# Selective scan plus mixture of experts on one core: softplus moved from TensorE to VectorE, one state group kept in PSUM

## The reference, cut to what matters

```python
uo = x @ W_in.T;  u, o = uo[..., :256], uo[..., 256:]
u = silu(depthwise_conv4(u) + conv_b)
g = u @ W_gate.T                        # 64 delta_lo, 16 b, 16 c
delta = softplus(delta_lo @ W_delta.T + delta_bias)
A = -exp(A_log)
h = exp(A * delta_t) * h + (delta_t * u_t) * b_t     # 256 channels x 16 states, 256 positions
y_t = sum_s h * c_t
y = (y + D * u) * sigmoid(o) * o
x = x + y @ W_out.T
# second block: 8 experts, top 2 (softmax), SwiGLU of width 176, and a shared SwiGLU of width 352
```

## Time and profile before

| | |
|---|---|
| median of 3 runs | 1453.29 us (1452.8 to 1456.53) |
| the profiled execution | 1453.74 us, its span 1451.6 us |
| mean granted TensorE clock | 0.961 of full speed |
| busy: TensorE, VectorE, ScalarE, GpSimd | 1273.9, 1042.5, 1080.1, 1219.0 us |
| period of a full step | 41.47 us (scan(7) starts at 640.42 and again at 681.89) |
| full steps (k = 2 to 29) | 28 |

### The profile page before, as it was taken

The page is one execution under the profiler, slowest core; times in us unless marked ns, Lnnn a source line. Parts: engine busy times, 40 slices in busy tenths (PEclk is TensorE's granted clock), DMA queues, the critical chain, the costliest instruction groups (busy, mean ns, idle before and its releaser), DMA issues.

```text
span 1451.6 us, 26176 instructions
## 1 busy us (share of the span) xinstructions
PE 1273.9 (88%) x9203; PEld 950.7 (65%) x9203; DVE 1042.5 (72%) x1664; ACT 1080.1 (74%) x2219; POOL 1219.0 (84%) x568
## 2 busy tenths in 40 slices
PE   3455999999999999999999999999999999998888
PEld 2223766777667667776676677766766777665677
DVE  2245778877777788777777887777778877776753
ACT  3777778777877787778777877787778777876642
POOL 3299898898889988988899889888998898899920
PEclk8667999999999999999999999999999999999989
DMA  3433322333333223333332233333322333233000
GB/s 102 103 89 84 92 67 69 95 96 92 74 86 95 65 70 96 96 93 75 84 94 66 70 96 96 92 74 85 95 65 69 96 97 92 69 83 89 7 5 8
DMA packets 71486, 115.08 MB, mean 79 GB/s; under 512 B 8174, under 2 KB 30396, under 8 KB 71356
## 3 DMA queue, kind: packets, MB, share of 16 engines
q1 hardware_dynamic: 67180, 110.71, 30.2%
q10 hardware_dynamic: 4176, 2.70, 0.6%
HBM read 41.04 MB, written 5.24 MB: 32 GB/s over the span
## 4 chain that ended last, share of the span: by engine, by line
PE 34%; DVE 22%; ACT 17%; issue 16%; POOL 1%; DVEq 0%; SPq 0%; DMA 0%; ACTq 0%; POOLq 0%
DVE state L648 11%; PE work_ps L864 10%; PE work_ps L873 10%; ACT decay_ps L451 6%; DVE features L666 5%; PE acc_ps L898 4%; ACT L483 3%; ACT L504 3%; PE acc_ps L856 3%; ACT L548 3%; PE work_ps L1081 2%; PE work_ps L997 2%; PE work_ps L927 2%; ACT u L526 2%; DVE features L658 2%
## 5 line engine op out<-in xcount | busy, mean ns | idle before, releaser
L393 POOL TENSOR_TENSOR read<-state,bc 128x1024 f32<-128x1024 f32 x256 | 605.6, 2379 | 93.0 <-DVE state L648 87.6
L384 POOL TENSOR_TENSOR inject<-rep,bc 128x1024 f32<-128x1024 f32 x256 | 604.4, 2385 | 52.2 <-DMA rep<-dd 52.2
L648 DVE TENSOR_TENSOR_SCAN state<-decay_ps,inject 128x1024 f32<-128x1024 f32 x256 | 580.9, 2280 | 48.3 <-ACT decay_ps L451 29.5
L451 ACT ACTIVATE decay_ps<-rep,neg_a 128x255 f32<-128x255 f32 x1024 | 423.5, 462 | 14.6 <-DVE state L648 5.5
L442 ACT ACTIVATE g_silu<-work_ps 128x512 f32<-128x512 f32 x224 | 133.9, 598 | 204.3 <-PE work_ps L864 204.0
L658 DVE TENSOR_TENSOR features<-g_silu,work_ps 128x512 f32<-128x512 f32 x224 | 151.6, 678 | 147.5 <-PE work_ps L873 107.5
L898 PE MATMUL acc_ps<-ffn_down,features 128*128 128x128 f32 (+1 forms) x1792 | 252.5, 284 | 0.0
L898 PEld LDWEIGHTS acc_ps<-ffn_down,features 128*128 128x128 f32 (+1 forms) x1792 | 217.2, 191 | 30.1 <-issue 12.3
L864 PE MATMUL work_ps<-xn2T_part,ffn_gate 128*128 128x256 f32 x1344 | 210.9, 294 | 2.5 <-ACT combT L499 1.8
L873 PE MATMUL work_ps<-xn2T_part,ffn_up 128*128 128x256 f32 x1344 | 207.7, 291 | 1.4 <-ACT dd L536 1.4
L856 PE MATMUL acc_ps<-read,sum_sel 128*32 128x256 f32 x2048 | 168.3, 401 | 37.8 <-POOL read L393 37.6
(11 more groups left out here) (134 smaller groups left out, 1398.5 us busy)
## 6 DMA issues: line engine op xcount, KB each, us to landing
rep<-dd SPq DMA_DIRECT2D x256, 256.0 KB, 4.8
bc<-bc_rows SPq DMA_DIRECT2D x64, 512.0 KB, 4.8
x_in<-in_L_attn_x_dram SPq DMA_DIRECT2D x32, 128.0 KB, 2.2
out_dram<-result SPq DMA_DIRECT2D x32, 128.0 KB, 1.8
bc_rows<-g_sb SPq DMA_DIRECT2D x32, 32.0 KB
state<-in_L_ffn_w_gate_dram ACTq DMA_DIRECT2D x1, 704.0 KB, 4.4
read<-in_L_ffn_w_up_dram ACTq DMA_DIRECT2D x1, 704.0 KB, 5.9
ffn_down<-in_L_ffn_w_down_dram ACTq DMA_DIRECT2D x1, 704.0 KB, 7.1
```

Source lines behind the costliest of these rows:

```text
L384: pool.tensor_tensor(inject[:, at % RI], du_all, b_all, ALU.mult).then_inc(inject_done, 1)
L393: pool.tensor_tensor(read[:, at % RR], state[:, at % RS], c_all, ALU.mult).then_inc(read_done, 1)
L451: last = act.activation(decay_ps[:, at % 2, j, 1:T], rep[n % 2][:, half * JB + j, 0, 1:T], ACT.Exp, scale=neg_a[:, col:col + 1])
L648: dve.tensor_tensor_scan(state[:, at % RS].rearrange("p j t -> p (j t)"), decay_ps[:, at % 2].rearrange("p j t -> p (j t)"), inject[:, at ...
```

## The change

1. **Softplus.** The bias becomes a row of `wdelta`, met by a row of ones in `g_sb`. ScalarE makes |z| in one instruction, then e and 1 + e right behind it, ahead of `decays(k, 6)`. relu(z) and (1 + e) - 1 are no longer made by ScalarE. VectorE makes, between weigh 3 and scan(6), max(z, 0) + e in PSUM and from it `z_less` = ((1 + e) - 1) - (max(z, 0) + e). In the next step ScalarE's logarithm goes straight into `delta_ps`, and VectorE subtracts `z_less` ahead of the product with u. TensorE's four products are gone.
2. **Group 4.** Its scan writes into `decay_ps` in place; VectorE itself multiplies by c (`read_own_group`), straight behind scan(4), and then clears the four first columns that the scan overwrote. GpSimd reads seven groups.
3. **Pair 2** stands ahead of scan(1) on VectorE.
4. `rep` has three buffers of half a sequence in place of two of a whole one; SyncE waits for the decays and injects of each half's buffer. TensorE and SyncE wait for `du_done` beside `dd_done`.

```diff
-                    dve.tensor_tensor_scan(state[:, at % RS].rearrange("p j t -> p (j t)"),
-                                           decay_ps[:, at % 2].rearrange("p j t -> p (j t)"),
+                    decays = decay_ps[:, at % 2].rearrange("p j t -> p (j t)")
+                    if q == OWN:
+                        to = decays
+                    else:
+                        dve.wait_ge(read_done, count(others(k, q) - RS + 1))
+                        to = state[:, others(k, q) % RS].rearrange("p j t -> p (j t)")
+                    dve.tensor_tensor_scan(to, decays,
...
+                def read_own_group():
+                    dve.wait_ge(c_in, 16 * (k + 1))
+                    dve.wait_ge(state_done, GROUPS * k + OWN + 1)
+                    dve.wait_ge(sum_done, count(GROUPS * (k - 1) + OWN + 1))
+                    c_all = bc[k % 2][:, 1, OWN % SG, :].unsqueeze(1).broadcast_to([P, JB, T])
+                    dve.tensor_tensor(read_own[:], decay_ps[:, OWN % 2], c_all, ALU.mult).then_inc(read_own_done, 1)
+                    dve.wait_ge(read_own_done, k + 1)
+                    dve.memset(decay_ps[:, OWN % 2, :, 0:1], 0.0).then_inc(decay_zero, 1)
...
+                pairs(2)
                 if on(0):
                     scan(1)
-                pairs(2)
...
                 if on(0):
                     scan(4)
+                    read_own_group()
                 if on(1):
                     n = k + 1
-                    dve.wait_ge(delta_mm, n + 1)
+                    dve.wait_ge(z_log_done, n + 1)
+                    dve.wait_ge(z_less_done, n + 1)
+                    dve.tensor_tensor(delta_ps, delta_ps, z_less[:], ALU.subtract).then_inc(delta_done, 1)
+                    dve.wait_ge(delta_done, n + 1)
...
+                if on(2):
+                    n = k + 2
+                    dve.wait_ge(z_exp_done, n + 1)
+                    dve.scalar_tensor_tensor(out=z_ps, in0=z_ps, scalar=0.0, in1=z_e[:], op0=ALU.max,
+                                             op1=ALU.add).then_inc(z_sum_done, 1)
+                    dve.wait_ge(z_sum_done, n + 1)
+                    dve.wait_ge(z_one_done, n + 1)
+                    dve.wait_ge(delta_done, n)
+                    dve.scalar_tensor_tensor(out=z_less[:], in0=z_w[:], scalar=1.0, in1=z_ps, op0=ALU.subtract,
+                                             op1=ALU.subtract).then_inc(z_less_done, 1)
                 if on(0):
                     scan(6)
...
-                reads(2, 3, 4)
+                reads(2, 3)
...
-                    act.activation(z_w[:], z_w[:], ACT.Ln).then_inc(z_log_done, 1)
+                    act.wait_ge(du_done, n)
+                    if on(-1):
+                        act.wait_ge(x1_done, k)
+                    act.activation(delta_ps, z_w[:], ACT.Ln).then_inc(z_log_done, 1)
...
                 if on(0):
                     decays(k, 5)
-                    decays(k, 6)
...
+                    act.activation(z_e[:], z_ps, ACT.Abs).then_inc(z_abs_done, 1)
+                    act.wait_ge(z_abs_done, n + 1)
+                    act.activation(z_e[:], z_e[:], ACT.Exp, scale=-1.0).then_inc(z_exp_done, 1)
+                    act.wait_ge(z_exp_done, n + 1)
...
+                    act.activation(z_w[:], z_e[:], ACT.Identity, bias=1.0).then_inc(z_one_done, 1)
+                if on(0):
+                    decays(k, 6)
                     decays(k, 7)
```

More of the change, by code:

```diff
@@ L72, in build @@
         read = sb("read", [P, RR, JB, T])
-        rep = [sb(f"rep{i}", [P, HALVES * JB, 2, T]) for i in range(2)]
+        read_own = sb("read_own", [P, JB, T])
+        rep = [sb(f"rep{i}", [P, JB, 2, T]) for i in range(RP)]
         scratch = features[:].rearrange("p c t -> p (c t)")
@@ L381, in inject_group @@
                     pool.wait_ge(state_done, count(at - RI + 1))
-                    du_all = rep[n % 2][:, half * JB:(half + 1) * JB, 1, :]
+                    du_all = rep[(HALVES * n + half) % RP][:, :, 1, :]
                     b_all = bc[n % 2][:, 0, g, :].unsqueeze(1).broadcast_to([P, JB, T])
@@ L447, in decays @@
                     act.wait_ge(rep_in[half], 16 * JB * (n + 1))
-                    act.wait_ge(state_done, count(at - 1))
+                    if q == OWN + 2:
+                        act.wait_ge(decay_zero, n + 2)
+                    else:
+                        act.wait_ge(state_done, count(at - 1))
                     for j in range(JB):
                         col = (g * HALVES + half) * JB + j
-                        last = act.activation(decay_ps[:, at % 2, j, 1:T], rep[n % 2][:, half * JB + j, 0, 1:T], ACT.Exp,
+                        last = act.activation(decay_ps[:, at % 2, j, 1:T], rep[(HALVES * n + half) % RP][:, j, 0, 1:T], ACT.Exp,
                                               scale=neg_a[:, col:col + 1])
@@ L853, in sum_states @@
                                   skip_group_check=True)
-                    pe.wait_ge(read_done, at + 1)
+                    if q == OWN:
+                        pe.wait_ge(read_own_done, n + 1)
+                        products = read_own
+                    else:
+                        pe.wait_ge(read_done, others(n, q) + 1)
+                        products = read[:, others(n, q) % RR]
                     for j in range(JB):
-                        last = pe.matmul(y_ps[j * CB:(j + 1) * CB, :], sum_sel[:], read[:, at % RR, j, :],
+                        last = pe.matmul(y_ps[j * CB:(j + 1) * CB, :], sum_sel[:], products[:, j, :],
                                          start=False, stop=(g == SG - 1), skip_group_check=True)
@@ L1029, in body @@
                     for half in range(HALVES):
-                        last = pe.matmul(z_ps[:, half, :], wdelta[:, half, :], g_sb[0:RANK, :], start=True, stop=True)
+                        last = pe.matmul(z_ps[:, half, :], wdelta[:, half, :], g_sb[:], start=True, stop=True)
                     last.then_inc(z_mm, 1)
```

114 lines of the change are left out of this document (46 added, 68 removed).

## The result

The changed kernel takes 1533.12 us (median of 4 runs, 1528.37 to 1534.66) against 1454.91 us (1452.8 to 1458.4, 4 runs): a ratio of 1.0532, interval [1.0505, 1.0559]. It is slower, as forecast, and 3 us above the top of the range (1474 to 1530).

What follows compares the result with a forecast made beforehand. Bound: a loop through VectorE and TensorE, no single engine. A step gains -0.05 + 1.31, about 1.25 us; times 28 is +35, start -6, giving 1482; the clock's 20 us makes 1502, range 1474 to 1530.

Steps and rivals of the forecast that it cites:

- The loop: Chain through VectorE and TensorE from one scan(7) to the next; an edit is worth what it does to it.
- The clock's term: Low clock behind scan(7) in an estimated one step in four: 0.7 us a step, 20 us in all.
- Pair 2: On VectorE ahead of scan(1): scan(2) gains 0.91 us, at least 0.8, and TensorE's wait for L927 goes.
- Own read, clearing, subtraction: On VectorE before delta*u: 1.20, 0.07 and 0.69 us, using up the gain and wait; ups(4) 0.05 us earlier.
- The two sums: On VectorE between weigh 3 and scan(6), a stretch without a hole: 0.69 us each, 1.31 us added.
- Rival C: Sums or own read on VectorE cost more than a product, at the scan's rate: 1513 to 1544; chance 0.08.
- Case A: TensorE's clock stays up in the loop: 1482 us (1472 to 1490); chance 0.34.
- Start: First three deltas, without TensorE's four products and GpSimd's read: 2 us each, -6 (between -3 and -10).
- The two waits of TensorE: Before the convolution, low clock costing 0 to 0.5 us; behind scan(7), waits of 1.3 and 0.6 us.
- The Trainium skill's account of idle gaps: Idle gaps drop TensorE to half rate; taken for every step, 28 times 2.85 us above 1482, or 1562.
- D: TensorE is the bound, before the convolution and u's product: -2.4 us a step, 1381 us; chance 0.09.
- E: The edits cancel: scan(5) comes 1.2 us earlier because `dd` is ready sooner, 1450 to 1457; chance 0.05.

Runs made afterwards that it cites:

- small_sums: The changed kernel with softplus' two sums on VectorE cut to 8 of 512 columns: 1478.93 us.
- fill2: The changed kernel plus four matmuls on zeros a step in TensorE's wait behind scan(6) and scan(7): 1487.37 us.
- fill123: As fill12, plus four more matmuls on zeros, three behind sum 2 and one behind the product of u: 1486.88 us.
- ps_fill2: The changed kernel with group 4 read by GpSimd as before, plus the matmuls of fill2: 1469.34 us.
- s_only: The changed kernel with group 4 read by GpSimd and pair 2 behind scan(1), as before, so softplus alone: 1536.0 us.
- fill12: As fill2, plus seven more matmuls on zeros in TensorE's waits before the convolution: 1512.84 us.

## Why the prediction was right or wrong

The loop and the cost of each edit in it came as worked out. The clock's term was too small by more than half, and with it the time lies above the range.

**Pair 2: right.** Said 0.91 us for scan(2), measured 1.02 (17.65 to 16.63), and 0.94 a step when it is the only edit.

**Own read, clearing, subtraction: right.** Said 1.20 + 0.07 + 0.69 with `dd` 0.05 us earlier. The lines by form of the changed kernel, 500 to 1000 us:

```profile
L674 DVE TENSOR_TENSOR read_own<-decay_ps,bc 128x1024 f32<-128x1024 f32 x11 | 13.5, 1225 | 1.3 <-issue 0.4
...
L826 DVE SCALAR_TENSOR_TENSOR work_ps<-work_ps,z_e 128x512 f32<-128x512 f32 x11 | 7.6, 693 | 0.0
L831 DVE SCALAR_TENSOR_TENSOR z_less<-z_w,work_ps 128x512 f32<-128x512 f32 x11 | 7.5, 686 | 0.4
```

The product out of PSUM takes 1225 ns, and delta*u starts 0.03 us earlier (25.78 against 25.81). The Trainium skill (VectorE: DVE Perf Modes, "The TRN2 errata — SBUF-src ops pay a fixed extra latency per instruction") gives the fp32 sum of two tensors as (N + 151) / 0.96 ns, which is 1224 for N = 1024; the trace of this product, which reads one side out of PSUM, agrees with its 1225.

**The two sums: right.** Said 0.69 each and 1.31 in the loop. They take 693 and 686 ns, and 1.34 us in the loop from scan(5) to scan(6), of which 1.01 left the step with all but 8 columns (small_sums). The step without clock effects was said to be 42.7 and is 42.76 to 42.81: the shortest of the changed kernel, and the means of fill2 and fill123. Rival C, the scan's rate, is refuted. Case A would have needed this step 28 times, and fill123 is that case on the chip: 1487 us, 5 above the 1482 of A.

**Start: near.** Said -6, measured -4.6.

**The two waits of TensorE: right in place and size.** Behind scan(7) said 1.3 and 0.6, measured 1.20 and 0.56 (0.64 us of sum between). Before the convolution the clock does fall. Said 0 to 0.5 us; in the changed kernel it costs nothing (fill2 and fill123, both 42.81), without the own read it goes with steps about 1 us longer (ps_fill2, 42.66 against 41.69).

**The step that failed** is the clock's term of the sum, which was mis-sized: "In which steps it falls the rows don't tell; as an estimate, one in four, which is 0.7 us a step and 20 us in all". The 2.85 us for a cold stretch was sized well, 3.16 measured (45.93 less 42.77). But it was every second step, and later every step at half the price (44.36 less 42.76 is 1.6). So the clock costs 1.68 us a step (44.44 less 42.76), in 28 steps 47 us, in place of 20; fill2 measures the same from the other side, 1533.12 less 1487.37 is 46. The share of one in four had no row behind it, and the sum without it, 1482, held to 5 us (fill123, 1487). The Trainium skill's account of idle gaps (TensorE: Matmul & The Clock Gate, "HAM oscillation"), whose own case has waits of some 3 to 5 us between bursts, gave 1562 when taken for every step; the truth was between it and my 1502, near the middle. The trace agrees that a wait can bring the low clock, with waits of only 1.20 and 0.56 us, but not that it does so each time.

**Sum.** 28 times 1.29 (42.76 less 41.47) is 36, 28 times 1.68 is 47, less 4.6 at the start: 78 us, and the medians differ by 78.2. That it fits so closely is in part luck: the steps are read from the traced executions, whose spans differ by 75.0, and in them all 31 intervals together are 79.8 us longer, where 28 times 2.97 counts 83.

**The other rivals.** D (TensorE the bound, 1381) falls by s_only, and the convolution in the changed kernel still waits 1.82 us for VectorE. E (cancelling) needed scan(5) 1.2 us earlier; it starts 34.71 us behind scan(7) in both kernels (640.42 to 675.13, 670.70 to 705.41).

**What is shown and what is open.** Shown: the softplus on VectorE makes the kernel slow; its 1.3 us are the work, and in the changed kernel the rest is TensorE's clock behind scan(7), since zeros multiplied there take it away. Shown too: the own read is near nothing alone, and a full 1.06 us beside the softplus. Open: why the fall comes every second step, and later every step with a shorter low stretch and half the cost; and why waits of 0.33 and 0.55 us bring it in seven steps of 26. Taking the sums out of the wait's way by moving sum 6, rather than by filling, was not tried.

## What to carry to other kernels

Before you take matmuls off TensorE, mark where it waits and what runs right behind the wait: a few tenths of a microsecond more ahead of work that is in the loop can cost several times as much through the clock, and even matmuls on zeros can be worth their place. Price an edit alone and beside the others: a wait that hides one addition may not hide a second. And when a change is a bundle, run its parts: here the one line that moved pair 2 gave 1.6%, and the rest took 7% back.

## What the runs showed of the hardware that was not expected

- The granted clock fell to 0.50 behind waits of 1.20 and 0.56 us with a sum of 0.64 us between them, in every second step, with the same waits in the steps where it did not.
- A kernel with a higher mean clock can be slower: fill12, 0.940 and 1512.84 us, against fill2, 0.909 and 1487.37 us. A convolution at the low clock (4.61 against 3.13 us) was filling a wait of 1.43 us that stands behind it.
- Fewer matmuls, more time per matmul: 256 fewer in the changed kernel, 22 us less busy, 78 us longer.
